# An expert stage whose gate and up products are computed in seven block products instead of eight

## The reference

```python
h = layernorm(x) * (1 + cb) + sb                 # 2048 tokens of width 256
weights = router_weights(h, Wr, temperature)     # one weight per token and expert
gate = einsum('btd,edf->ebtf', h, Wg)            # each expert: 256 x 256
up   = einsum('btd,edf->ebtf', h, Wu)
# two of the eight experts have a low-rank product of 64 columns added to Wg, Wu and Wd
mid  = silu(gate) * up
out  = einsum('bte,ebtd->btd', weights, einsum('ebtf,efd->ebtd', mid, Wd))
x    = x + gb * out
```

## Time and profile before

| | |
|---|---|
| time, median of 3 runs | 804.85 us (803.84 to 805.88) |
| the profiled execution: its time, its span | 805.75 us, 804.0 us |
| PE busy, share of the span | 793.1 us, 99% |
| DVE, ACT, POOL busy | 508.3, 465.8, 403.3 us |
| granted clock of PE, mean | 0.998 of full speed |

### The profile page before, as it was taken

The page is one execution under the profiler, slowest core; times in us unless marked ns, Lnnn a source line. Parts: engine busy times, 40 slices in busy tenths (PEclk is TensorE's granted clock), DMA queues, the critical chain, the costliest instruction groups (busy, mean ns, idle before and its releaser), DMA issues.

```text
span 804.0 us, 14773 instructions
## 1 busy us (share of the span) xinstructions
PE 793.1 (99%) x5116; PEld 710.0 (88%) x5116; DVE 508.3 (63%) x1074; ACT 465.8 (58%) x1259; POOL 403.3 (50%) x547
## 2 busy tenths in 40 slices
PE   9899999999999999999999999999999999999997
PEld 8688899999999999999999999898888888888887
DVE  5667676475466667457557757666785454554575
ACT  5777677677577767767667866652553232332322
POOL 3767587486567567567657656220311010110493
PEclk9999999999999999999999999999999999999999
DMA  9200010000000000000000000202410110100002
GB/s 334 104 28 1 2 61 1 1 8 2 0 8 2 1 4 5 1 2 8 1 1 8 1 1 2 79 1 53 118 40 2 40 40 1 40 0 1 1 1 106
DMA packets 8329, 22.32 MB, mean 28 GB/s; under 512 B 1592, under 2 KB 4280, under 8 KB 8128
## 3 DMA queue, kind: packets, MB, share of 16 engines
q1 hardware_dynamic: 7680, 21.29, 7.9%
q10 hardware_dynamic: 576, 0.08, 0.1%
HBM read 19.26 MB, written 2.11 MB: 27 GB/s over the span
## 4 chain that ended last, share of the span: by engine, by line
PE 94%; DVE 2%; ACT 1%; issue 1%; POOL 1%; DMA 1%; ACTq 0%; DVEq 0%; POOLq 0%
PE ps_o L671 14%; PE ps_proj L548 9%; PE ps_proj L550 9%; PE ps_proj L549 9%; PE ps_s L548 7%; PE ps_s L549 7%; PE ps_s L550 7%; PE ps_turn L600 4%; PE ps_y L548 4%; PE ps_y L549 4%; PE ps_y L550 4%; PE ps_turn L618 3%; PE ps_turn L548 2%; PE ps_turn L549 2%; PE ps_turn L550 2%; PE ps_o L550 2%
## 5 line engine op out<-in xcount | busy, mean ns | idle before, releaser
L671 PE MATMUL ps_o<-vaug,probs 128*128 128x129 f32 x1024 | 136.1, 276 | 1.7 <-POOL probs L1674 0.9
L671 PEld LDWEIGHTS ps_o<-vaug,probs 128*128 128x128 f32 x1024 | 130.0, 192 | 8.0 <-POOL probs L1674 1.4
L993 ACT ACTIVATE ps_s<-ps_s,knorm 128x512 f32<-128x512 f32 x128 | 79.3, 657 | 96.2 <-PE ps_s L550 96.1
L1287 DVE RECIPROCAL rden<-ps_o 128x2 f32<-128x2 f32 x128 | 21.8, 170 | 155.5 <-PE ps_o L671 155.3
L1680 POOL TENSOR_TENSOR we_lo<-raw_e,we_hi 128x512 fp32r<-128x512 f32 x22 | 28.4, 1318 | 161.3 <-ACT we_hi L1036 161.3
L1257 DVE TENSOR_TENSOR prod<-ps_proj,cs 128x1024 f32<-128x1024 f32 x76 | 92.5, 1218 | 11.0 <-ACT sq L936 11.0
L1625 POOL TENSOR_TENSOR root<-ssq,powers 128x4 f32<-128x4 f32 x76 | 77.8, 1024 | 27.4 <-ACT sq L936 27.4
L936 ACT ACTIVATE sq<-ps_proj 128x128 f32<-128x128 f32 x304 | 80.1, 279 | 18.9 <-PE ps_proj L550 16.0
L1641 POOL TENSOR_TENSOR prod<-prod 128x512 f32<-128x512 f32 x62 | 80.1, 1292 | 10.0 <-DVE prod L1257 10.0
L548 PE MATMUL ps_proj<-w_hi,h_hi 128*128 128x512 f32 x192 | 83.3, 434 | 0.4 <-DVE h_lo L1204 0.4
L1672 POOL TENSOR_SCALAR_AFFINE_SELECT probs<-probs 128x256 f32<-128x256 f32 x64 | 26.4, 412 | 106.7 <-ACT probs L1001 106.4
(11 more groups left out here) (220 smaller groups left out, 2191.2 us busy)
## 6 DMA issues: line engine op xcount, KB each, us to landing
raw_e<-in_we SPq DMA_DIRECT2D x8, 768.0 KB, 4.4
raw_p<-in_wqkv SPq DMA_DIRECT2D x6, 512.0 KB, 8.5
raw_e<-in_wo SPq DMA_DIRECT2D x4, 512.0 KB, 12.7
x_all<-in_x SPq DMA_DIRECT2D x1, 1536.0 KB, 7.3
out<-acc SPq DMA_DIRECT2D x3, 512.0 KB, 2.6
x_all<-in_wmod SPq DMA_DIRECT2D x1, 1024.0 KB, 10.4
gates_a<-gate_rows_dram SPq DMA_DIRECT2D x8, 128.0 KB, 2.9
gates_b<-gate_rows_dram SPq DMA_DIRECT2D x1, 1024.0 KB, 10.2
```

The costliest lines, as they stand in the source:

```text
L671: mm = pe.matmul(ps_o[:, h * (D + 1):(h + 1) * (D + 1)], probs[:, s % 2, at:at + P], vaug[b % 2][:, k, i // 2, :], start=(h == 0 and k == ...
L993: act.activation(ps_s[:, t, :], ps_s[:, t, :], ACT.Tanh, scale=knorm[:, b % 2, t, i // 2:i // 2 + 1]).then_inc(tanh_done, 1)
```

## The change

For tiles 8 to 27 the gate product, and for tiles 12 to 27 the up product too, is cut into a 2 x 2 by 2 x 2 block product: the weights (256 x 256) into A11, A12, A21, A22 of 128 x 128, the tokens (256 x 512) into B11 to B22 of 128 x 256. A plain product of these takes eight block products. The changed kernel takes seven, of blocks and of sums of blocks (T1 to T4 of the tokens, S1 to S4 of the weights), and adds the results in several places.

- PE: 21 matmuls of 256 columns in place of 12 of 512 columns, for each gate or up product of a tile. Four block products go first (`seven_first`, `up_first`), the other three are added onto two PSUM banks after ACT has copied these banks to SBUF (`seven_last`, `up_rest`).
- ACT: two copies of 128 x 512 per product of a tile (`copy_seven`, `copy_up`), silu in two pieces of 256 and 768 columns (`silu_seven`), and the hi parts of the sums (`round_t`, `round_s`).
- POOL: three sums of 128 x 256 per product of a tile (`sums_seven`, `sums_up`), the sums of tokens once per block of 512 tokens (`sums_t`, `rest_t`), the sums of weights once per expert (`sums_s`, `rest_s`).
- DVE: one sum of 128 x 512 per product of a tile (`add_quarters`, `add_up`). From tile 12 on the product of silu and up is one of 256 columns and one of 768 columns (`product_both`); the second reads both its inputs from SBUF.
- The token blocks 4 and 5 are written to DRAM by ACT's queue and read back into `h2_back` by SP's, since their place is taken over.
- The low-rank steps, the last block's router and the pieces of `split_e` move to other steps, and some buffers to other addresses. `part` gets three buffers, and its wait on `final_add` goes.

The core of the diff:

```diff
+            def seven_first(m):
...
+                product_of(ps_s[:, 0, 0:S], of["A11"], of["B11"], True)
+                product_of(ps_s[:, 0, S:], of["S2"], of["T2"], False).then_inc(seven_ready, 1)
+                if q:
+                    pe.wait_ge(quarters_added, q)
+                product_of(ps_s[:, 1, 0:S], of["S1"], of["T1"], True)
+                product_of(ps_s[:, 1, S:], of["S3"], of["T3"], False).then_inc(seven_ready, 1)
+            def seven_last(m):
...
+                pe.wait_ge(seven_copied, 2 * q + 1)
+                product_of(ps_s[:, 0, 0:S], of["A12"], of["B21"], False).then_inc(gu_ready, 1)
+                pe.wait_ge(seven_copied, 2 * q + 2)
+                product_of(ps_s[:, 1, 0:S], of["S4"], of["B22"], False)
+                product_of(ps_s[:, 1, S:], of["A22"], of["-T4"], False).then_inc(gu_ready, 1)
...
+            for m in range(SEVEN, EIGHT):
+                seven_first(m)
+                if m < BOTH:
+                    up_alone(m)
+                    seven_last(m)
+                else:
+                    up_first(m)
+                    seven_last(m)
+                    up_rest(m)
+                down(2 * m - 2)
+                down(2 * m - 1)
...
+            def round_t(n):
+                act.wait_ge(t_made, 4 * n + 4)
...
+                elif n == 2:
+                    act.wait_ge(t_split, 4)
...
+            for m in range(SEVEN, EIGHT):
+                copy_seven(m)
+                if m >= BOTH:
+                    copy_up(m)
+                for e, m3 in SEVEN_SPLIT.get(m, ()):
                     split_e(e, m3)
+                if m in SEVEN_ROUND:
+                    round_s(SEVEN_ROUND[m])
+                if m == SEVEN + 2:
+                    round_t(3)
+                silu_seven(m)
+                mid_head(2 * m)
+                mid_head(2 * m + 1)
...
+            def product_both(m):
...
+                dve.tensor_tensor(mid[:, 0, 0:S], ps_proj[:, 0, 0:S], silu[:, 0, 0:S], ALU.mult).then_inc(mid_done, 1)
+                dve.wait_ge(quarter_silu, 2 * (m - SEVEN) + 2)
+                dve.wait_ge(up_last, m - BOTH + 1)
+                dve.wait_ge(up_added, m - BOTH + 1)
+                dve.tensor_tensor(flat(mid)[:, S:], up_quarters[:].rearrange("p a n -> p (a n)")[:, S:], flat(silu)[:, S:], ALU.mult).then_inc(mid_done, 1)
...
+            def sums_up(m):
+                qq = m - BOTH
+                pool.wait_ge(up_copied, 2 * qq + 1)
+                pool.tensor_tensor(up_seven[:, 0, :], up_seven[:, 0, :], up_seven[:, 1, :], ALU.add).then_inc(up_u_made, 1)
+                pool.wait_ge(up_copied, 2 * qq + 2)
+                pool.tensor_tensor(up_seven[:, 2, :], up_seven[:, 2, :], up_seven[:, 3, :], ALU.add).then_inc(up_pair_made, 1)
...
+                pool.tensor_tensor(up_quarters[:, 3, :], up_seven[:, 0, :], up_seven[:, 2, :], ALU.add).then_inc(up_last, 1)
...
+            rest_s(NL)
+            low_rest(1)
+            rest_t(0)
+            split_e(NL, 1)
+            rest_t(1)
+            for m in range(SEVEN, EIGHT):
+                sums_seven(m)
+                if m >= BOTH:
+                    sums_up(m)
```

More of the change, by code:

```diff
@@ L522, in _ @@
             sp.wait_ge(router, 2 * STEPS)
+            for kept in h2_kept:
+                sp.wait_ge(kept, 16)
             expert(1)
@@ L846, in _ @@
                 slot(s)
-            for m in range(NEXT, len(TILES)):
+            for m in range(NEXT, SEVEN):
                 up(2 * m)
@@ new lines, in copy_seven @@
+            def copy_seven(m):
+                q = m - SEVEN
+                if q == 0:
+                    act.wait_ge(h2_turned, B)
+                    act.wait_ge(y_gated, B)
+                else:
+                    act.wait_ge(last_quarter, q)
+                    act.wait_ge(quarters_added, q)
+                for bank in range(2):
+                    act.wait_ge(seven_ready, 2 * q + bank + 1)
+                    act.activation(seven[:, 2 * bank:2 * bank + 2, :].rearrange("p a n -> p (a n)"), ps_s[:, bank, :], ACT.Copy).then_inc(seven_copied, 1)
@@ L1585, in _ @@
                         route(LATE, piece)
+            for m in range(SEVEN, EIGHT):
+                add_quarters(m)
+                if m < BOTH:
+                    for g in (2 * m, 2 * m + 1):
+                        product_seven(g)
+                else:
+                    add_up(m)
+                    product_both(m)
+                for g in (2 * m, 2 * m + 1):
+                    mid_tail(g)
+                accumulate(2 * m - 2)
+                accumulate(2 * m - 1)
+                for i in LOW_STEPS.get(m, ()):
+                    fold(i)
+            for m in range(EIGHT, len(TILES)):
+                product(2 * m)
+                product(2 * m + 1)
+                mid_tail(2 * m)
+                mid_tail(2 * m + 1)
+                accumulate(2 * m - 2)
+                accumulate(2 * m - 1)
             accumulate(2 * len(TILES) - 2)
@@ new lines, in _ @@
+            inv_std2(B - 1)
+            low_rest(0)
+            pool.wait_ge(h2_split, B)
+            sums_t(2)
+            split_e(NL, 0)
+            sums_s(NL)
+            rest_s(NL)
+            low_rest(1)
+            rest_t(0)
+            split_e(NL, 1)
+            rest_t(1)
+            for m in range(SEVEN, EIGHT):
+                sums_seven(m)
+                if m >= BOTH:
+                    sums_up(m)
+                if m == SEVEN:
+                    split_e(NL, 2)
+                    rest_t(2)
+                if m == SEVEN + 1:
+                    sums_t(3)
+                if m in SEVEN_ROUND:
+                    rest_s(SEVEN_ROUND[m])
+                for e, m3 in SEVEN_SPLIT.get(m, ()):
```

295 lines of the change are left out of this document (270 added, 25 removed).

## The result

The changed kernel takes 816.58 us (median of 5 runs, 814.43 to 817.34), the kernel before 804.85 beside it: the ratio is 1.014 [1.0124, 1.0156]. It is 1.4% slower, which is more than the runs differ among themselves, and 9.8 us above the 806.8 that was forecast; it also lies above the range (797.5 to 814.5). The profiled execution has a span of 814.3 us against 804.0.

The account below looks back on a forecast made before the run. PE's own list bounds the kernel before; after the change a ring through ACT, POOL and DVE does. Tiles 12 to 23 +2.0, tiles 24 to 27 -1.3, start +1.2: +1.9 on 804.85 gives 806.8 us, range 797.5 to 814.5.

Parts of the forecast that it names:

- the chain ahead of tile 8: Expert 2's split, sums and rests on POOL and ACT make PE wait 2.3 us at tile 8, DVE contention included.
- The two waits that the chain did have: At tile 8 PE waits 0.5 us for POOL's first rests, then 1.3 us and a little more for ACT's copies.
- the start is worse or better: Rival, 0.10: slower sums or DVE's router steps make PE wait 5 us ahead of tile 8, 809.5 us; if faster, 804.5.
- The ring: Per step from tile 12: copy, six sums, product, two `mid_hi`, copy; 7.2 us undisturbed, 8.66 on average with POOL/DVE collisions.
- The long turn of the four: Of an expert's four steps, the one with POOL's four sums of weights: ring 9.0 us, the others 8.54.
- the term 2.0: Tiles 12 to 23: 12 x 8.66 = 103.9 against 100.7 us, less 1.2 us that the ring starts ahead: +2.0 us.
- PE waits in most steps: Sign: PE waits for ACT's `seven` in most steps from 12 to 24, 0.6 to 1.1 us each, not in 25 and 26.
- three free steps in the sum: Tiles 24 to 27: 8.54 + 3 x 7.92 = 32.3 us against 33.6, so -1.3 us.
- PE's part: Matmuls of 256 columns cost 0.12 us; a step with both products changed takes 7.92 us of PE, 0.47 less than 8.39.
- PE rules after all: Rival, 0.30: every step from 12 on is 7.92 us; 798.5 us, or 796.2 if the chain ahead of tile 8 doesn't bind.
- The lock is the bound: Rival, 0.18: POOL and DVE instructions with SBUF inputs add in full, 8.8 to 9.2 us a step; 814 to 818 us.

Follow-up runs that it names:

- x6: Changed kernel with POOL's subtractions for expert 2's pieces and expert 3's low-rank A cut to 4 columns per row, order kept: 812.25 us.
- x3: Changed kernel with the last block's router pieces earlier: piece 1 on ACT, pieces 3 to 6 on DVE from tile 7's step into tile 6's: 812.13 us.
- x9: Kernel with both cures, its start reordered on DVE, POOL and ACT, with router pieces 3 to 6 behind tile 7's first product: 807.06 us.
- x5: Changed kernel with ACT writing the silu of the last three quarters to PSUM, so DVE's last products have one SBUF input: 806.19 us.
- both cures: Changed kernel with the router's pieces early on ACT and DVE and the silu in PSUM: 802.17 us, ratio 0.9961 to the kernel before.
- x15: Kernel with both cures, POOL's low-rank rests moved into idle time in step 6, second token rests ahead of expert 2's second piece: 802.33 us.

## Why the prediction was wrong

**The step that failed** is in the part on the sum: the chain ahead of tile 8, "With the contention of DVE I take 2.3 us". It measured 9.9 us, and that is 7.6 of the 9.8 us by which the forecast missed. POOL's and ACT's part of that chain was right: POOL's last rest ahead of tile 8 was forecast to end at 598.4 and ended at 598.3. What I didn't do is to follow DVE's list beside it. I had found that POOL and DVE exclude each other, and had priced it for the product and the `mid_lo` in every step. But in the one place where POOL works for 12 us nearly without a break I put it down as a lump. DVE has 19 small router instructions there, ahead of two things that PE waits for. Their own lengths are 1.4 of 5.3 us in the first group and, by the estimate above, 3.3 of 6.1 in the second; the rest is waiting, up to one POOL instruction each. Three of the four that waited in the first group have two inputs in SBUF, the kind that the prediction had priced. x6 and x3 each take about 4 us of this out, one by POOL's work and the other by DVE's place, and with the order of x9 the router's pieces are blocked again. How the second wait divides between the contention and the place of the thirteen stays open, since x6 left it at 3.4 us. The third part of the 9.9, 3.2 us of lower clock behind the two waits, I hadn't counted at all. The two waits that the chain did have (0.5 us for POOL's rests, 1.3 for ACT's copies) don't show in the changed kernel, because PE comes too late for them.

The rival *the start is worse or better* had this mechanism by name ("DVE's router steps hold them up"), at 5 us and with 0.10. It was the right mechanism at half its size.

**The ring** was right as a mechanism, and shown by x5: free the product of POOL, and 10.4 us come back. Its size was a little low: 8.66 forecast, 8.79 measured. The long turn of the four is 9.62 and not 9.0 (the copies of tiles 18 and 19 start at 689.45 and 699.07): behind the four sums of weights POOL's first sum starts 1.44 us after the copy, and the product of the same turn takes its full 1.99 us, where I had let it lose less. Tiles 12 to 23 came to +3.4 us against the term 2.0, tiles 24 to 27 to -0.7 against -1.3, and this is the rest of the miss. That PE waits in most steps by 0.6 to 1.1 us was nearly so: nine waits, 6.9 us, the longest 1.4. The product took 1.97 us (forecast 2.1), and POOL was busy for 544.9 us (forecast over 500). Steps 26 and 27 run free, at 7.78 and 7.80, and step 25 takes 8.44; I had said 25 and 26, and had three free steps in the sum.

**PE's part** held. Matmuls of 256 columns cost 0.118 to 0.12, a step with both products and no waits 7.8 us (forecast 7.92), one with the gate alone 8.1. *PE rules after all* was not the case in the changed kernel, but it is nearly the case in x5, whose 7.91 per step is what that rival had.

**The other rivals.** *The lock is the bound* named 814 to 818, where the time came out, but by 8.9 to 9.2 us in each step; PE's steps are 8.56. The time fell into it by luck, for another reason. (Its upper end is off by one: 9.2 us a step gives 819 by its own terms.)

**What stays open** is the start: with both cures steps 7 and 8 still take 23.5 us where their matmuls need 17.9. Moving POOL's block, in x15, only changed what it meets; whether DVE's list would be too long there even without contention isn't shown. A start at a tile where no router is left wasn't tried.

## What to carry to other kernels

Where two engines exclude each other, walk through both of their lists side by side, at the place where one works without a break, and charge each small instruction there that can be kept waiting with up to the length of its neighbour; its own length says little. Look first at what decides the exclusion (here, where an instruction's second input lies): changing that gave 10 us, where waits and reorderings moved the collision elsewhere. And a long wait of PE can cost more than itself, here 1.6 us after 3 us of waiting, though nothing after one of 2.5 us in x15.

## What the runs showed of the hardware

**Engines also wait for each other where the program doesn't say so.** The section on the chip says that they wait only through semaphores. The five router instructions above wait for no semaphore of POOL's, and took 5.30 us beside it against 1.4.

**Instructions that read one SBUF tensor can be kept waiting by POOL too.** I had taken only those with two inputs. In the changed kernel the TENSOR_SCALAR of 4 columns at 591.79 took 1.08 us beside POOL, 0.17 in the kernel before; TENSOR_REDUCE (0.19 at 591.56) and RECIPROCAL (0.18 at 601.47 and 604.28) were no longer beside POOL than alone. The sign was already in the trace of before: its TENSOR_SCALAR of 32 columns took 1.13 us while POOL worked, and 0.24 in the changed kernel with POOL at rest. DVE, then POOL, before:

```profile
578.63 1.13 DVE L1436 TENSOR_SCALAR r_a<-r_log,r_s 128x32 f32<-128x32 f32 x1
...
577.88 1.84 POOL L1749 TENSOR_TENSOR lowB_lo<-lowB,lowB_hi 128x768 fp32r<-128x768 f32 x1
```

The Trainium skill (SBUF — State Buffer, "Who interferes with whom") says it: `tensor_scalar` may run in a mode that uses the pair of ports shared with GpSimd, and `tensor_reduce` on this chip never does. These rows agree. In x15 this kind of wait decides: the two TENSOR_SCALARs shown there take 0.78 and 1.50 us.

**A product with its second input in PSUM isn't kept waiting.** L1656 took 678 to 681 ns in all sixteen steps of x5, with POOL at work beside it as in the changed kernel.

**PE's clock fell after some single waits, and not by their length alone.** After the waits of 3.4 and 3.0 us matmuls of 256 columns were 0.21 us apart in place of 0.12 for a time. In x3 the same came after a shorter one, of 1.8 us in step 8, but not after the 1.3 us in step 7. In x15 it did not come after 2.5 us in step 7, and came after 3.2 us in step 8. In the ring of the changed kernel, with a wait of 1.4 us at 664.5, it did not. What decides isn't shown. Stretches of x3 behind its two waits (the clock is the third number from the end):

```profile
591.92:596.00 4.08, 3.98 (x32) 3.80 (x33) 4.03 (x8) 2.64 (x5) 4.00 (x4) 1.00 0.00 0
601.90:606.20 4.30, 4.26 (x21) 4.12 (x22) 3.63 (x9) 1.23 (x3) 4.10 (x5) 0.60 0.00 0
```

Of x15 behind its two:

```profile
593.22:599.00 5.78, 5.78 (x45) 5.60 (x46) 5.70 (x10) 4.34 (x9) 3.97 (x4) 1.00 0.02 4
605.19:609.50 4.31, 4.31 (x23) 4.31 (x24) 3.24 (x7) 1.63 (x3) 0.01 (x1) 0.60 0.26 107
```

And of the changed kernel around the wait in the ring:

```profile
661.00:667.00 6.00, 4.61 (x38) 4.34 (x37) 5.30 (x8) 3.89 (x8) 5.28 (x5) 1.00 0.00 0
```
